# Two places for the input tile, and a reordered passage from the second dense layer into the small model

## The reference

```python
x = layernorm(x + x @ w_masked.T)                      # weight masked by 32x32 blocks
x = layernorm(x + x @ W.T + bias + lora(x))            # adapter chosen by sequence
x = layernorm(x + small_model(x))                      # Win, 4 blocks, Wout
x = layernorm(x + x @ W3.T + b3 + mixture(x))          # 8 experts, routed by sequence

# one block of the small model, on 128 features
y = silu(layernorm(h) * w + b)
h = h + sconv(y) * sc_lin      # a complex first-order recurrence along the sequence
y = layernorm(h) * w + b
h = h + silu(y @ W1.T + b1) @ W2.T + b2
```

## Time and profile before

| | |
|---|---|
| median of three runs | 1725.62 us |
| the profiled execution | 1723.15 us |
| its span in the trace | 1720.9 us |
| PE busy | 1659.3 us, 96% |
| DVE busy | 1051.5 us, 61% |
| ACT busy | 648.2 us, 38% |
| POOL busy | 442.5 us, 26% |
| share of the DMA engines, 1300 to 1420 us | 0.57 |

### The profile page before, as it was taken

How to read it: one execution, slowest core, us unless ns; L and a number is a source line. 1 busy time by engine, 2 the same in 40 slices (tenths; PEclk the granted TensorE clock), 3 DMA queues, 4 the chain that set the end, 5 groups by cost and what they waited for, 6 DMA issues and landing times.

```text
span 1720.9 us, 22743 instructions
## 1 busy us (share of the span) xinstructions
PE 1659.3 (96%) x8002; PEld 1336.9 (78%) x8002; DVE 1051.5 (61%) x1993; ACT 648.2 (38%) x937; POOL 442.5 (26%) x377
## 2 busy tenths in 40 slices
PE   6999999999999999999889999999799999999998
PEld 5788888888888888888766666676577778878886
DVE  6434444335555555557667877777867776777633
ACT  2434333333333333322334555454433333433321
POOL 4111111100000000000366777773323222211200
PEclk9999999999999999999879999999799999999999
DMA  6224333333333333323140000002455556545321
GB/s 258 110 98 147 113 107 112 123 123 119 111 111 116 115 104 114 112 106 105 58 156 25 1 1 1 1 1 100 151 169 189 167 201 212 186 170 195 131 89 61
DMA packets 72688, 196.57 MB, mean 114 GB/s; under 512 B 8834, under 2 KB 17026, under 8 KB 72322
## 3 DMA queue, kind: packets, MB, share of 16 engines
q1 hardware_dynamic: 51842, 125.92, 22.0%
q10 hardware_dynamic: 20736, 69.22, 10.1%
HBM read 122.75 MB, written 72.35 MB: 113 GB/s over the span
## 4 chain that ended last, share of the span: by engine, by line
PE 84%; DVE 5%; issue 4%; DMA 3%; ACT 2%; POOL 1%; ACTq 0%; SPq 0%; POOLq 0%; DVEq 0%
PE ps L680 19%; PE ps L682 19%; PE ps L681 19%; PE ps L887 6%; PE ps L694 3%; PE ps L829 3%; PE ps L787 2%; PE ps L835 2%; PE ps L879 1%; PE ps L878 1%; PE ps L877 1%; DMA x_in<-x_scratch 1%; PE ps L855 1%; PE ps L736 1%; DMA x_scratch<-cx 1%
## 5 line engine op out<-in xcount | busy, mean ns | idle before, releaser
L680 PE MATMUL ps<-wall_x,x_hi 128*128 128x512 f32 x1008 | 399.4, 396 | 8.3 <-DVE wall_x L1411 3.7
L681 PE MATMUL ps<-wall_x,x_hi 128*128 128x512 f32 x1008 | 394.3, 391 | 0.0
L682 PE MATMUL ps<-wall_x,x_lo 128*128 128x512 f32 x1008 | 394.1, 391 | 0.0
L2052 POOL TENSOR_TENSOR rstd<-var_eps,minus_half 128x1 f32<-128x1 f32 x96 | 79.9, 833 | 897.1 <-DVE minus_mean L1446 897.1
L1437 DVE BATCH_NORM_STATS2 stats<-row 128x6 f32<-128x512 f32 x192 | 133.0, 694 | 176.0 <-ACT row L1096 171.6
L680 PEld LDWEIGHTS ps<-wall_x,x_hi 128*128 128x128 f32 x1008 | 190.2, 189 | 50.6 <-issue 7.5
L682 PEld LDWEIGHTS ps<-wall_x,x_lo 128*128 128x128 f32 x1008 | 190.2, 189 | 40.5
L681 PEld LDWEIGHTS ps<-wall_x,x_hi 128*128 128x128 f32 x1008 | 190.4, 189 | 37.7
L680 PE MATMUL ps<-wall_y,x_hi 128*128 128x512 f32 x512 | 202.4, 395 | 0.0
L682 PE MATMUL ps<-wall_y,x_lo 128*128 128x512 f32 x512 | 199.6, 390 | 0.0
L681 PE MATMUL ps<-wall_y,x_hi 128*128 128x512 f32 x512 | 199.4, 389 | 0.0
(11 more groups left out here) (259 smaller groups left out, 2827.0 us busy)
## 6 DMA issues: line engine op xcount, KB each, us to landing
x_scratch<-row ACTq DMA_DIRECT2D x64, 512.0 KB, 2.8
x_in<-x_scratch SPq DMA_DIRECT2D x64, 512.0 KB, 3.7
w_first<-in_w_t SPq DMA_DIRECT2D x64, 256.0 KB, 3.0
out<-row ACTq DMA_DIRECT2D x32, 512.0 KB, 2.6
x_in<-in_x_t SPq DMA_DIRECT2D x29, 512.0 KB, 3.3
cx<-x_scratch SPq DMA_DIRECT2D x24, 512.0 KB, 4.2
x_scratch<-cx ACTq DMA_DIRECT2D x24, 512.0 KB, 4.0
w_in<-in_w_t SPq DMA_DIRECT2D x32, 256.0 KB, 3.0
```

What stands on the lines that cost most here:

```text
L680: pe.matmul(bank, hi[:, k], wall[:, k, 0, cols], start=(k == 0), stop=False)
L681: pe.matmul(bank, hi[:, k], wall[:, k, 1, cols], start=False, stop=False)
L682: return pe.matmul(bank, lo[:, k], wall[:, k, 0, cols], start=False, stop=(k == KC - 1))
L2052: pool.tensor_tensor(rstd[:, i:i + 1], var_eps[:, i:i + 1], minus_half[:, 0:1], ALU.pow)\
```

## The change

1. `x_in` becomes two places. Odd tiles stay at the old one, even tiles get new memory. Each has its own semaphore. `load_x` waits for the tile two before to be turned (or split) instead of the one before, and SP's steps call it one tile further ahead, `load_x(s + 3)` where `load_x(s + 2)` stood.
2. Inside the second half of tile 63's product, PE turns tile 62 after four of the eight chunks and takes the variance of unit 2 after seven. Before, both stood behind the product, variance first.
3. DVE makes the scans of unit 0, reads the variance of unit 2 and rotates unit 1 before it splits tile 62 and before it takes the second half of tile 63. POOL's two turns back of unit 0 come before the root of tile 63.
4. `mixes()` moves from the end of turn 3 into the first layer (step 8), to memory of its own.

The core of the diff, in the order memory, SP, PE (`product`), DVE (from `if s == 8` on), POOL (`rotate_back`):

```diff
+def x_loads(s):
+    return (s - FIRST) // 2 + 1
...
-    mix = at("mix", M, [P, LAYERS, P])
+    mix = at("mix", FACTOR + 12288, [P, LAYERS, P])
...
-    x_in = at("x_in", Z, [P, D])
+    x_in = [at("x_in0", FACTOR + 8192, [P, D]), at("x_in1", Z, [P, D])]
...
-                if s > B_END or A_END < s < B_END:
-                    sp.wait_ge(x_turned, s - A_END)
-                elif s > FIRST:
-                    sp.wait_ge(hi_ready, s)
-                    sp.wait_ge(lo_ready, s)
+                if s - 2 >= A_END:
+                    sp.wait_ge(x_turned, s - 1 - A_END)
+                elif s - 2 >= FIRST:
+                    sp.wait_ge(hi_ready, s - 1)
+                    sp.wait_ge(lo_ready, s - 1)
...
-                    if s == B_END:
+                    if s == B_END + 1:
                         sp.wait_ge(y_rotated[0], MLP_END)
                         sp.wait_ge(y_rotated[1], MLP_END)
...
             load_x(FIRST)
+            load_x(FIRST + 1)
...
                     load_x(p + 3)
+                    load_x(p + 4)
                 for s in range(p + 2 if b == 0 else p, p + TPB):
                     j = s % TPB
-                    load_x(s + 2)
+                    load_x(s + 3)
...
+                if s == B_END - 1:
+                    product(s, 1, range(4))
+                    turn_y(s - 1)
+                    product(s, 1, range(4, 7))
+                    variance1(EARLY - 1)
+                    product(s, 1, range(7, KC))
+                    continue
...
+                if s == 8:
+                    mixes()
...
+                if s == B_END - 1:
+                    scan(0)(0)
+                    take_var1(EARLY - 1)
+                    scan(1)(0)
+                    rotate(1)
+                    split_y(s - 1)
+                    continue
...
             half_stats(B_END - 1, 1)
             aggregate(B_END - 1)
-            scan(0)(0)
-            scan(1)(0)
-            rotate(1)
...
                 if turn == EARLY:
-                    mixes()
                     split_w1(0)
...
+                if s == B_END - 2:
+                    rotate_back(0)(0)
+                    rotate_back(1)(0)
             for turn in range(EARLY, TURNS):
-                turn_of(order[:3], turn)
+                turn_of(order[2:3] if turn == EARLY else order[:3], turn)
```

More of the change, by code:

```diff
@@ L351, in build @@
         centre_ready, bias_done, dve_done = sem("centre_ready"), sem("bias_done"), sem("dve_done")
-        x_loaded, x_turned = sem("x_loaded"), sem("x_turned")
+        x_loaded, x_turned = [sem(f"x_loaded{i}") for i in range(2)], sem("x_turned")
         hi_ready, lo_ready, mm_done = sem("hi_ready"), sem("lo_ready"), sem("mm_done")
@@ L481, in load_x @@
                     sp.wait_ge(stored[i % 2], 16 * (i // 2 + 1))
-                    sp.dma_start(x_in[:], x1[i]).then_inc(x_loaded, 16)
+                    sp.dma_start(x_in[s % 2][:], x1[i]).then_inc(x_loaded[s % 2], 16)
                 elif s >= B_END:
                     c = s - B_END
-                    if s == B_END:
+                    if s == B_END + 1:
                         sp.wait_ge(y_rotated[0], MLP_END)
@@ L488, in load_x @@
                     sp.wait_ge(c_stored[c_slot(c)], 16 * c_uses(c))
-                    sp.dma_start(x_in[:], x3[c]).then_inc(x_loaded, 16)
+                    sp.dma_start(x_in[s % 2][:], x3[c]).then_inc(x_loaded[s % 2], 16)
                 else:
-                    sp.dma_start(x_in[:], a["x_t"][s]).then_inc(x_loaded, 16)
+                    sp.dma_start(x_in[s % 2][:], a["x_t"][s]).then_inc(x_loaded[s % 2], 16)
             def load_w(n):
@@ L581, in _ @@
                         load_w(PARTS * (b + 1) + 2 * j + i)
-                if s + 2 < B_END:
-                    load_x(s + 2)
+                if s + 3 < B_END:
+                    load_x(s + 3)
                 if b + 1 == BATCHES and j == 0:
@@ L684, in turn_x @@
             def turn_x(s):
-                pe.wait_ge(x_loaded, 16 * (s - FIRST + 1))
+                pe.wait_ge(x_loaded[s % 2], 16 * x_loads(s))
                 pe.wait_ge(hi_ready, s)
@@ L693, in turn_x @@
                 for k in range(KC):
-                    last = pe.transpose(ps_x[:, k * P:(k + 1) * P], x_in[:, k * P:(k + 1) * P], ident[:])
+                    last = pe.transpose(ps_x[:, k * P:(k + 1) * P], x_in[s % 2][:, k * P:(k + 1) * P], ident[:])
                 last.then_inc(x_turned, 1)
@@ L1081, in split_x @@
                 elif s < A_END:
-                    act.wait_ge(x_loaded, 16 * (s - FIRST + 1))
-                    src = x_in[:]
+                    act.wait_ge(x_loaded[s % 2], 16 * x_loads(s))
+                    src = x_in[s % 2][:]
                 else:
@@ L1414, in split_x @@
             def split_x(s):
-                src = x_first[:, s] if s < FIRST else x_in[:] if s < A_END else ps_x
+                src = x_first[:, s] if s < FIRST else x_in[s % 2][:] if s < A_END else ps_x
                 hi, lo = [flat(t) for t in x_parts(s)]
```

## The result

| | before | after |
|---|---|---|
| median, six runs each on one chip | 1722.22 us | 1712.18 us (1709.83 to 1713.78) |
| ratio | 1 | 0.9932, 95% interval 0.9918 to 0.9945 |
| the profiled execution, its span | 1723.15, 1720.9 | 1709.83, 1707.6 |
| median of all runs in this study | 1722.8 (56 runs) | 1713.2 (16 runs) |

The change makes the kernel 0.6% faster by the medians, 10.0 us by the first runs and 9.6 by all of them. It gives 0.7%, since one run of before took 1728.99 us. The forecast was 1718.1, with a range that ended at 1712.5. It was too high by 5.9 us.

A forecast was written before the change was run, and what follows sets the result against it. PE, busy 96% of the span, was taken as the bound. Loads 5.3 + matrices 2.2 + reordering and clock 0 = 7.5 us off 1723.15 gave 1715.6; the median's 2.5 more made 1718.1, range 1712.5 to 1723.5.

The forecast's parts named there:

- The base: Whole kernel: the median of the runs, 1725.62 us, 2.5 above the profiled execution, from which the gain was taken.
- Loads: Last layer: a second input place removes four waits of the turn for `x_in`, gaining 5.3 us.
- Mix matrices: Passage: making the matrices in the first layer takes 2.8 us off the chain, 2.2 us net.
- The 0.6 us held back beside `y_rot`: Passage: DVE's scan meets the end of POOL's `y_rot` pair and loses about 0.6 us of the matrices' 2.8.
- Scans sooner, turn inside the product: Around tile 63's product: the reordering brings tile 63's turn no sooner; gain 0, ends -0.7 and +0.9 us.
- Clock: Passage, 27 us at 1.2 GHz: an earlier rise could gain 1 to 3 us or lose the same; booked 0.
- the rival with the clock: Passage and model's exit: the clock rises sooner as well, 7.5 + 3 us gained, 1715.1 us; chance 21%.
- two idle pieces of PE: Passage: PE idled 3.53 and 2.80 us before two short pieces, after which the clock was at 1.2 GHz.

The follow-up runs named there:

- second and third profile of after: The changed kernel, unedited, run and profiled again in two further jobs: medians 1714.04 and 1713.38 us, ratios 0.9948 and 0.9942.
- only the input places: The kernel before with two places of `x_in` and the loads one tile further ahead, nothing else: ratio 0.9968, 1717.14 us.
- the edit that moved both roots: The changed kernel with DVE's first variance of unit 2 behind the split of tile 62, POOL's order unchanged: ratio 0.9940, 1712.67 us.
- the gaps filled: The changed kernel with 28 unread product-sized matmuls in PE's three gaps of the passage: ratio 0.9926, 1710.84 us.
- the step further: The changed kernel with unit 2's variance after tile 62's split, POOL's rotations before its root; here plus 21 matmuls in PE's gaps: 0.9931, 1710.53 us.

## Why the prediction was wrong

Two steps failed, the base in size and the zero for the reordering in mechanism. The 5.9 us of the miss are 1725.62 - 1722.22 = 3.4 in the base, and 2.5 in the gain (10.0 against 7.5).

- **The base.** The forecast put the sum on the median of three runs, 2.5 us above the profiled execution. Over 56 runs the kernel before has 1722.8, and the profiled 1723.15 was the better base by far. The three runs lay between 1721.69 and 1728.99. This is the largest part of the miss.
- **Loads, 5.3.** Right: 5.5 by ratio, 6.0 in the trace.
- **Mix matrices, 2.2.** Right: 2.29. The 0.6 us held back beside `y_rot` was 0.5. The scan was held beside POOL (1.78, 1.27 without), the scaling that reads PSUM was not (0.67, 0.68 without). By the rule of the Trainium skill that the forecast cited ("SBUF — State Buffer", section "SBUF: two separate sides") the scan is held and the scaling is not, and the trace agrees.
- **Scans sooner, turn inside the product, booked at 0.** This is the step whose mechanism failed. It had the statistics right (no sooner: 11.16 against 11.13) and named both numbers of the root, 1.51 and about 0.6. It then set the gain aside because the root stands behind POOL's turned-back pair, which would end at 854.0. By the forecast's own numbers that is no reason: in the kernel before the root had started at 854.20, so it could start in its old place and end 0.9 sooner. So it was. The pair ended at 854.12, and `var_eps` at 854.34: the pair was not in the way. The root started in its old place (11.39 us from the scaling, before 11.37) and took 0.96 us less, with the turn behind it 0.94 sooner, and the variance of unit 0 gained another 0.2: 1.2 us, a little over the upper end of 0.9 that stood in the range. That the turn inside the product is worth nothing was right.
- **Clock, booked at 0.** The remainder: 10.0 - 5.5 - 2.3 - 1.2 = 1.0 us. Part of it is luck: three of the first six runs fell in the group with the higher clock, of all sixteen only five. By all runs it is 9.6 - 9.0 = 0.6, within the noise. By places, the three profiles of after gain 3.96, -0.04 and 0.36 us on before between the variance and the eleventh mix. So the rival with the clock (1715.1), which gave it 3 us, is right for one way in which the program runs and not for the usual one. The low stretch does end sooner. Counted from the scaling it lasts from 8.3 to 35.6 us before, and in the second and third profile of after from 8.4 to 32.3 and from 11.1 to 31.6. Its start is no sign of the change: only the input places, with the passage as before, has 11.1 to 35.0. The forecast also read the fall as coming after two idle pieces of PE (3.53 and 2.80 us). The clock fell at 851.2 us, inside the first, and the second lies in the low stretch.

The chances had 0.58 for no measurable change and 0.40 for faster; it was faster. The measured 1712.18 lies 0.3 us below the range. With the profile's own time as base and 1.2 for the reordering, the same working gives 1723.15 - 8.7 = 1714.5, 2.3 us above the result.

**What stays open.** No run changes alone whether a scan is under way at the root of tile 63. That a scan holds the root rests on the four traces in which this root was held, on the many roots of four columns, and on the edit that moved both roots. What decides in which of its two ways the program meets the clock's steps is open. And why a higher clock in the passage with the gaps filled (0.94, and 0.87 in the step further) shows so little in the time of the whole was not taken apart further.

## What to carry to other kernels

Follow a stall to the end of the last instruction that it delays, on the engine that is late: here DVE's results came no sooner, but the one that POOL made from them did, because it no longer met a scan. Count places from one instruction that all versions share; that separates the order of the work (good to 0.02 us here) from the clock, which moves the same program by 3 to 4 us. And put a forecast on the profiled execution's own time where the median rests on three runs only: here that median was 2.8 us above the one of 56.

## What the runs showed of the hardware

- Which of two operations on DVE and POOL starts first by 0.1 us decides a microsecond. A root of one column takes 0.55 us if it starts 0.09 to 0.13 ahead of a scan, and 1.46 to 1.51 if it starts 0.10 to 0.18 behind one. The scan itself took 1.28 to 1.30 in either case. A root of four columns takes 1.01 alone and 1.91 to 1.96 if it starts behind a scan's start.
- One program has two groups of times, some 3.6 us apart, that differ in the mean granted clock: 0.986 (median 1710.2) and 0.982 to 0.984 (median 1713.8). Three profiles of it agree in their places to 0.02 us up to the variance of unit 0.
- 28 matmuls more, 7 us of work in PE's gaps, raised the clock in that stretch from 0.68 to 0.94 and made the kernel no slower: 1710.84 against 1712.18.
